# Attention and feed-forward on one core: the prologue's bias load, its stores and the second batch's projections are put in another order

## The chip, the core and the metric

One core of a Trainium2 chip runs the whole kernel. The metric is the device time of one execution in microseconds (us). The engines are TensorE (PE; the load of its weights is PEld), VectorE (DVE), ScalarE (ACT), GpSimd (POOL) and SyncE (SP), each with an instruction queue of its own; SP, ACT and POOL also issue DMAs.

## The reference

Two sequences (B = 2) of 1024 rows of 128 numbers pass a pre-norm attention with 16 heads of 8 and a feed-forward of 512, all in 32-bit floats:

```python
x = x + attn(layernorm(x))
x = x + ffn(layernorm(x))
def attn(x):
    q, k, v = x @ Wq.T + bq, x @ Wk.T + bk, x @ Wv.T + bv
    sim = einsum('bhid,bhjd->bhij', q, k) + rel_emb[bucket(i - j)] * SCALE
    sim = where(j > i, -inf, sim)
    return einsum('bhij,bhjd->bhid', softmax(sim), v) @ Wo.T + bo
def ffn(x):
    y = x + relu(x @ w1[0] + b1[0]) @ w2[0] + b2[0]
    return layernorm(y) * gamma + beta
```

The bias of a score depends only on i - j and the head, by a table of 32 buckets.

## The kernel before

**Groups and steps.** The work is cut into 8 groups g of 4 heads (4 groups of each batch), and a group into 12 steps. A step takes one block of 128 keys against up to 512 queries: `scores` (keys times queries), `biases` (adds the near biases TT), an exponential on ACT (line 743), and `values`, which sums probabilities times values on TensorE. The softmax's maxima must be known before a group's scores, so each group also has 42 jobs, its "units". A unit multiplies queries by keys on TensorE (line 1130); DVE then takes the maximum of each row, far units by `TENSOR_REDUCE` (line 883), near units with the bias table NBH added (line 890, one instruction and a short read-out for each head). Units 16 and 41 are "m" units: TensorE turns the maxima of half a group (line 1116), DVE copies them out (`mrow`, line 878), and SP moves them by a DMA into the operand QA (`move_m`, line 462). The first scores of a half wait for that DMA. Units use three banks of PSUM in turn, so TensorE can be up to three units ahead of DVE. The units of group g + 1 stand between the steps of group g. Group 0 has no group before it: its first units (OWN0 of them) run ahead of the first scores.

**Prologue of batch 0.** The order of each engine is written out by hand, in the program's text. DVE and ACT normalise 4 tiles of 128 rows at a time (`stats0`, `deviation`, `norm`), TensorE turns them (`task_t`, line 1046), ACT copies them back (`turned`, line 676), TensorE multiplies by Wq and Wk (`task_qk`, line 1052) and Wv (`task_v`, line 1058). Each query and key is kept as three bf16 parts: ACT writes the first part (`first_parts`, line 681), DVE forms the remainder, the second part and the third (`split`, lines 830, 832, 835); for the first 512 queries POOL forms the third (line 591). SP stores the parts to DRAM (`store` and `store_keys`, lines 445 and 454); from there `load_q` (SP, lines 408 and 412) and `load_k` (POOL or ACT, lines 420 and 424) load them in the layout of the units, QA and KA. A pair (b, c) is batch b, half c of its 1024 rows; all five stores of a pair count on one semaphore, s_qst[b][c].

**Biases.** `task_f` multiplies the table by one-hot rows into one bank, `bias_table` on DVE makes of it the reversed biases Fr and the two parts F16. SP stores both. ACT loads them back as `rev` (1 MB, in the tile PT, line 713) and `TL` (two transfers of 480 KB, in the tile OT, line 716). Eight `task_flip` turn `rev` into NBH by way of ACT and DVE (`copy_nbh`, lines 696 and 851); `copy_tt` on ACT makes TT of TL (line 705).

**Batch 1.** POOL normalises it (`second_batch_norm`, lines 574 to 579). Its projections stand between the first 17 units of group 0, Q and K of one half together (T_AT, QK_AT, V_AT). ACT writes its first parts and the whole values (line 684), POOL splits those (lines 608 to 612). They are stored on SP and first loaded for group 4. `keep_busy` multiplies zeros on TensorE, in three places: before the table, before the first turn, and 12 of them ahead of the first scores (line 1282).

## Time and profile before

| what | us |
|---|---|
| median of 3 runs | 344.32 (344.03 to 344.61) |
| profiled execution, whole | 342.63 |
| profiled execution, span | 340.8 |
| TensorE busy | 286.3 (84% of the span) |
| VectorE busy | 272.6 (80%) |
| ScalarE busy | 190.3 (56%) |
| GpSimd busy | 92.0 (27%) |

A span runs from the first to the last instruction; the execution's own time adds what lies around it. Shares are means over stages that have different limits, so a stage is read from its own stretch. A row of the chain names, for a stretch of time, the work that the last instruction hung on; a row of the timeline names when an engine or queue started something, how long it took and, in brackets, how long the engine had been idle before and what ended that. SPq, ACTq and POOLq are the DMA issues of an engine's queue: their time is that of issuing, not of moving.

### The profile page before, as it was taken

The page shows a single profiled execution, that of the slowest core. Times are in us where ns is not written, and L with a number is a line of the kernel's source. Part 1 is how long each engine was busy: PE and PEld are TensorE (multiplying, and loading weights), DVE is VectorE, ACT ScalarE, POOL GpSimd, SP SyncE. Part 2 cuts the span into 40 slices and gives each one's busy share as a digit, 9 for nine tenths or more (in the row PEclk, how much of TensorE's full clock was granted, in tenths as well). Part 3 has the DMA queues.
Part 4 walks back from the last instruction along what each step waited for, and adds up shares of the span by engine and source line. Part 5 has one row for each costly group of instructions (what it writes and reads, how often), then busy time and mean ns, then how long its engine had stood idle before and what let it go on. Part 6 is the DMA issues. An engine that isn't in the chain of part 4 may idle for free.

```text
span 340.8 us, 8308 instructions
## 1 busy us (share of the span) xinstructions
PE 286.3 (84%) x3224; PEld 129.0 (38%) x3224; DVE 272.6 (80%) x967; ACT 190.3 (56%) x264; POOL 92.0 (27%) x138
## 2 busy tenths in 40 slices
PE   8492987769998989998898999889899988999880
PEld 4151342222343344334334334423432443367650
DVE  5653556989899888988888989888899957838894
ACT  2433544386558556755766674685575468843230
POOL 6109999602020220201022022001200001615351
PEclk9967698969999999999999999999999999999997
DMA  7475417001010120102022222114221002000022
GB/s 217 131 205 145 132 38 236 17 2 38 21 56 4 56 56 3 53 7 57 0 57 56 34 64 55 35 25 87 56 34 26 9 14 37 4 4 13 0 63 62
DMA packets 16263, 18.80 MB, mean 55 GB/s; under 512 B 4576, under 2 KB 11872, under 8 KB 16096
## 3 DMA queue, kind: packets, MB, share of 16 engines
q1 hardware_dynamic: 13168, 12.10, 14.6%
q0 software_dynamic: 2400, 3.45, 3.5%
q10 hardware_dynamic: 656, 2.73, 2.7%
q8 instruction: 25, 0.41, 0.5%
q14 instruction: 14, 0.11, 0.1%
HBM read 11.81 MB, written 4.23 MB: 47 GB/s over the span
## 4 chain that ended last, share of the span: by engine, by line
PE 52%; DVE 22%; ACT 11%; issue 6%; DMA 4%; POOL 3%; SPq 1%; DVEq 0%; POOLq 0%
PE ps L1174 15%; PE ps L1130 12%; ACT PT L743 9%; DVE FM L883 8%; PE ps L1145 8%; PE ps L1162 7%; DVE junk L890 4%; PE ps L1052 3%; DMA qk_scratch<-QS 2%; PE ps L1207 2%; DVE st L947 2%; DVE U L1000 1%; PE ps L1116 1%; PE ps L1077 1%; DVE xnT L913 1%
## 5 line engine op out<-in xcount | busy, mean ns | idle before, releaser
L743 ACT ACTIVATE PT<-ps 128x1024 f32<-128x1024 f32 (+1 forms) x192 | 144.7, 814 | 92.2 <-PE ps L1162 87.3
L883 DVE TENSOR_REDUCE FM<-ps 128x1 f32<-128x512 f32 (+2 forms) x192 | 109.1, 616 | 12.8 <-PE ps L1130 12.3
L890 DVE CUSTOM_DVE_ANT_0 junk<-ps,NBH 128x256 bf16<-128x256 f32 (+1 forms) x256 | 90.2, 399 | 23.5 <-PE ps L1130 23.5
L1130 PE MATMUL ps<-KA,QA 56*128 56x256 bf16 (+3 forms) x544 | 96.5, 288 | 14.7 <-DVE FM L883 7.4
L1145 PE MATMUL ps<-QA,KA 58*128 58x512 bf16 (+3 forms) x384 | 77.7, 333 | 17.6 <-ACT PT L743 14.6
L1174 PE MATMUL ps<-PT,VG 128*16 128x512 f32 (+3 forms) x768 | 86.1, 493 | 0.1
L1130 PEld LDWEIGHTS ps<-KA,QA 56*128 56x128 bf16 x544 | 33.3, 95 | 99.8 <-DVE FM L883 42.1
L420 POOL DMA_DIRECT2D KA<-qk_scratch x30 | 16.4, 550 | 163.3 <-PE ps L1162 151.9
L1145 PEld LDWEIGHTS ps<-QA,KA 58*128 58x128 bf16 x384 | 24.8, 94 | 37.4 <-ACT PT L743 30.4
L1162 PE MATMUL ps<-TT,flb 128*32 128x176 f16 (+4 forms) x1152 | 38.4, 243 | 0.0
L1162 PEld LDWEIGHTS ps<-TT,flb 128*32 128x32 bf16 x1152 | 21.3, 96 | 17.1 <-issue 15.5
L1174 PEld LDWEIGHTS ps<-PT,VG 128*16 128x16 f32 x768 | 21.5, 97 | 6.1 <-ACT OT L748 2.3
L890 DVE DVE_READ_ACCUMULATOR2_ANT FM<- 128x1 f32 x256 | 20.7, 81 | 0.0
L641 POOL TENSOR_SCALAR tmp<-mv 128x4 f32<-128x4 f32 x8 | 2.3, 290 | 66.7 <-DVE mv L950 66.7
L1207 PE MATMUL ps<-QS,late_s 128*128 128x512 f32 x32 | 15.8, 611 | 0.8 <-ACT QS L773 0.8
L424 POOL DMA_DIRECT2D KA<-qk_scratch x30 | 15.5, 528 | 0.0
L1052 PE MATMUL ps<-xnT,early_s 128*128 128x512 f32 x16 | 13.0, 958 | 1.9 <-ACT xnT L676 1.9
L936 DVE RECIPROCAL xnT<-xnT 128x256 f32<-128x256 f32 (+1 forms) x4 | 10.1, 2537 | 0.0
L681 ACT ACTIVATE QS<-ps,early_s 128x512 bf16<-128x512 f32 x8 | 5.5, 692 | 8.2 <-PE ps L1052 8.2
L956 DVE TENSOR_TENSOR QS<-ps,X 128x512 f32<-128x512 f32 x4 | 2.7, 682 | 8.5 <-PE ps L1198 8.5
L748 ACT COPY OT<-ps 128x512 f32<-128x512 f32 x16 | 9.5, 592 | 0.0
L1046 PE MATMUL ps<-early_s,XN 128*128 128x128 f32 x16 | 4.0, 396 | 6.3 <-DVE XN L820 4.2
(98 smaller groups left out, 256.2 us busy)
## 6 DMA issues: line engine op xcount, KB each, us to landing
QA<-qk_scratch SPq DMA_DIRECT2D x64, 48.0 KB
KA<-qk_scratch POOLq DMA_DIRECT2D x30, 96.0 KB, 2.6
qk_scratch<-QS SPq DMA_DIRECT2D x12, 128.0 KB
qk_scratch<-QS SPq DMA_DIRECT2D x8, 192.0 KB
X<-in_x SPq DMA_DIRECT2D x4, 256.0 KB, 5.1
PT<-fr_scratch ACTq DMA_DIRECT2D x1, 1024.0 KB, 5.6
out<-U SPq DMA_DIRECT2D x4, 256.0 KB, 2.3
OT<-f_scratch ACTq DMA_DIRECT2D x2, 480.0 KB, 8.3
```

The source lines that it names most:

```text
L420: eng.dma_start(KA[64 * e:64 * e + 48, p, c, :, :].rearrange("r h n -> r (h n)"), bass.AP(qk_d, at + e * TILE, [[LINE, 2 * HD], [0, NPART] ...
L424: eng.dma_start(KA[64 * e + 48:64 * e + KS, p, c, :, :].rearrange("r h n -> r (h n)"), bass.AP(qk_d, at + e * TILE + 2 * HD * LINE, [[LINE ...
L743: nc.scalar.activation(PT[:, s % 3, 2 * q:2 * q + 2, off:off + w], ST[:, q, :, off:off + w], ACT.Exp).then_inc(s_exp, 1)
L883: nc.vector.tensor_reduce(FM[:, ib, heads[0]:heads[-1] + 1:2, piece], bank[:, 0:w * len(heads)].rearrange("p (h n) -> p h n", n=w), AX.X, ...
L890: last = nc.vector.tensor_tensor_reduce(junk[:, n % NSM, i, 0:w], bank[:, i * w:(i + 1) * w], nb[:, h, 256 - w:256], 1.0, NEG, ALU.add, AL ...
L936: own2(nc.vector.reciprocal(den, den))
L1052: nc.tensor.matmul(ps[:, BANK["QK"[qk], b, c], :], (wq_s, wk_s)[qk][:, :], xnT[:, b, c * IC:(c + 1) * IC], start=True, stop=True).then_inc ...
L1130: last = nc.tensor.matmul(SM[:, n % NSM, i * w + j - j0:i * w + j - j0 + nj], QA[r0:r0 + KS, p, ib // 4, q, (ib % 4) * 128:(ib % 4 + 1) * ...
L1145: last = nc.tensor.matmul(ST[:, q, e, off:off + w], KA[64 * e:64 * e + KST, p, jb // 4, q, (jb % 4) * 128:(jb % 4 + 1) * 128], QA[64 * e:6 ...
L1162: last = nc.tensor.matmul(ST[r0:r0 + 32, q, h % 2, off:off + n], flb[:, 32 * e:32 * e + 32], TT[:, hg, h, u0:u0 + n], start=False, stop=Tr ...
L1174: last = nc.tensor.matmul(OV[32 * h:32 * h + 2 * HD, off:off + w], VG[:, jb, g, h, :], PT[:, s % 3, h, off:off + w], start=(jb == 0), stop ...
L1207: last = nc.tensor.matmul(bank, w1_s[:, f * 128:(f + 1) * 128], tT[:, c % 2, :], start=True, stop=True)
```

## The change

- Two banks take the two halves of the bias table; the reversed one is multiplied first, the other behind the first turn. SP stores Fr and at once loads `rev`, ahead of all stores of queries and keys. The three operations that make F16 go from DVE to POOL. TL is loaded by SP behind `load_q(0, 0, 1)`.
- s_qst is split into one semaphore for queries and one for keys. ACT stores the second and third parts of the first 512 keys; POOL forms the third part of both halves of queries of batch 0.
- TensorE's first three `task_f`, the flips, V of batch 0 and `keep_busy` are in another order, and more zeros are multiplied early (10, 5 and 4); the 12 ahead of the first scores are gone.
- POOL takes the root of all eight tiles of batch 1 at once. ACT writes only the whole values of batch 1's Q and K, and POOL makes the first part too.
- Batch 1's projections stand one by one between the units (BATCH1_AT). In group 0 the first m unit comes ahead of units 14 and 15, and 21 jobs instead of 17 stand before the first scores.

```diff
+def order_of(g):
+    ks = list(range(NU - 1))
+    if g == 0:
+        ks.remove(M0)
...
 def stream():
     out = []
     for g in range(G):
-        for k in range(NU - 1):
...
-T_AT = {2: 0, 8: 1}
-QK_AT = {4: 0, 10: 1}
-V_AT = {13: 0, 15: 1}
+BATCH1_AT = {7: ("T", 0), 9: ("Q", 0), 10: ("K", 0), 12: ("V", 0), 13: ("T", 1), 15: ("Q", 1), 16: ("K", 1), 18: ("V", 1)}
 RECIP_AFTER = (6, 14, 22, 30)
-OWN0 = 17
+OWN0 = 21
...
-        STORED = 16 * (HP + NPART)
+        STORED_Q, STORED_K = 16 * HP, 16 * NPART
...
+            at = (2 * c + 1) * SIDE + b * 2 * GPB * TILE + a * HD * LINE
+            eng.dma_start(bass.AP(qk_d, at, [[TILE, 2 * GPB], [IC, HD * HP], [1, IC]]),
+                          QS[:, b, 1, a, c * IC:(c + 1) * IC]).then_inc(s_qst[b][c][1], 16)
         @block.sync
...
+            sp.dma_start(rev[:, :], bass.AP(fr_d, 0, [[H, 128], [1, 256 * H]])).then_inc(s_rev, 16)
+            sp.wait_ge(s_q1, 2)
+            store_keys(sp, 0, 0, 0)
+            store(0, 0, 0)
             sp.wait_ge(s_f, 2)
             for part in range(2):
                 sp.dma_start(bass.AP(f16_d, part * BW * H, [[H, 128], [128 * H, XC], [1, H]]),
                              F16[:, part, :, :]).then_inc(s_fst[1], 16)
-            def key_part(c, a):
-                ready, count = ((s_q1, 2 * c + 2), (s_mid, 2 * c + 2), (s_q3[0][1], c + 1))[a]
-                sp.wait_ge(ready, count)
-                store_keys(0, c, a)
-            key_part(0, 0)
-            key_part(0, 1)
-            store(0, 0, 0)
-            key_part(0, 2)
-            sp.wait_ge(s_qst[0][0], STORED)
+            sp.wait_ge(s_qst[0][0][0], STORED_Q)
             load_q(sp, 0, 0, 0)
-            key_part(1, 0)
+            sp.wait_ge(s_q1, 4)
+            store_keys(sp, 0, 1, 0)
             store(0, 1, 0)
-            key_part(1, 1)
-            key_part(1, 2)
-            sp.wait_ge(s_qst[0][1], STORED)
+            sp.wait_ge(s_mid, 4)
+            store_keys(sp, 0, 1, 1)
+            sp.wait_ge(s_q3[0][1], 2)
+            store_keys(sp, 0, 1, 2)
+            sp.wait_ge(s_qst[0][1][0], STORED_Q)
             load_q(sp, 0, 0, 1)
+            sp.wait_ge(s_fst[1], 32)
+            for part in range(2):
+                sp.dma_start(TL[64 * part:64 * part + 64, :],
+                             bass.AP(f16_d, part * BW * H, [[H, 64], [1, NEARU * H]])).then_inc(s_tl, 16)
             load_q(sp, 1, 1, 0)
+            move_m(0, 0, 0)
             load_q(sp, 1, 1, 1)
-            move_m(0, 0, 0)
             sp.dma_start(late_s[:, :], late).then_inc(s_late, 16)
             for c in range(2):
                 for qk in range(2):
...
+                pool.wait_ge(s_var, 4)
+                nc.gpsimd.tensor_scalar(tmp4[:, 8:16], mv[:, 8:16, 1], EPS, None, ALU.add).then_inc(s_p1, 1)
+                pool.wait_ge(s_p1, 1)
+                nc.gpsimd.tensor_tensor(rs[:, 8:16], tmp4[:, 8:16], mhalf[:, :], ALU.pow).then_inc(s_p1, 1)
+                pool.wait_ge(s_p1, 2)
             def second_batch_norm(k):
...
+                pool.wait_ge(s_mid, 2 * c + 1)
+                q = QS[:, 0, 0, :, c * IC:(c + 1) * IC]
+                nc.gpsimd.tensor_tensor(q[:, 2, :], R[0][:, 2 * c, :], q[:, 1, :], ALU.subtract).then_inc(s_lo, 1)
             ones(0)
...
-            pool.wait_ge(s_mid, 1)
-            q = QS[:, 0, 0, :, 0:IC]
-            nc.gpsimd.tensor_tensor(q[:, 2, :], R[0][:, 0, :], q[:, 1, :], ALU.subtract).then_inc(s_lo, 1)
+            pool.wait_ge(s_ff, 1)
+            nc.gpsimd.tensor_copy(F16[:, 0, :, :], Ff[:, :, :]).then_inc(s_p3, 1)
+            pool.wait_ge(s_p3, 1)
+            nc.gpsimd.tensor_tensor(Ff[:, :, :], Ff[:, :, :], F16[:, 0, :, :], ALU.subtract).then_inc(s_p3, 1)
+            pool.wait_ge(s_p3, 2)
+            nc.gpsimd.tensor_scalar(F16[:, 1, :, :], Ff[:, :, :], LSC, None, ALU.mult).then_inc(s_f, 1)
+            queries_lo(0)
             pool.wait_ge(s_zero, 3)
-            pool.wait_ge(s_qst[0][0], STORED)
+            pool.wait_ge(s_p2, 1)
+            pool.wait_ge(s_qst[0][0][1], STORED_K)
             load_k(pool, 0, 0, 0, s_ldk)
-            pool.wait_ge(s_p2, 1)
+            queries_lo(1)
+            second_batch_deviation()
             second_batch_norm(2)
             second_batch_norm(3)
             pool.wait_ge(s_rows, 16)
             add_bv(0)
             load_k(pool, 1, 1, 0, s_ldk)
-            pool.wait_ge(s_qst[0][1], STORED)
...
                 c, qk = k // 2, k % 2
                 q = QS[:, 1, qk, :, c * IC:(c + 1) * IC]
                 pool.wait_ge(s_r, k + 1)
+                nc.gpsimd.tensor_copy(q[:, 0, :], R[1][:, k, :]).then_inc(s_p0, 1)
+                pool.wait_ge(s_p0, 3 * k + 1)
                 nc.gpsimd.tensor_tensor(R[1][:, k, :], R[1][:, k, :], q[:, 0, :], ALU.subtract).then_inc(s_p0, 1)
-                pool.wait_ge(s_p0, 2 * k + 1)
+                pool.wait_ge(s_p0, 3 * k + 2)
                 nc.gpsimd.tensor_copy(q[:, 1, :], R[1][:, k, :]).then_inc(s_p0, 1)
-                pool.wait_ge(s_p0, 2 * k + 2)
+                pool.wait_ge(s_p0, 3 * k + 3)
...
             act.wait_ge(s_early, 16)
-            first_parts(0, 0)
-            act.wait_ge(s_fst[0], 16)
-            act.dma_start(rev[:, :], bass.AP(fr_d, 0, [[H, 128], [1, 256 * H]])).then_inc(s_rev, 16)
-            act.wait_ge(s_fst[1], 32)
-            for part in range(2):
-                act.dma_start(TL[64 * part:64 * part + 64, :],
-                              bass.AP(f16_d, part * BW * H, [[H, 64], [1, NEARU * H]])).then_inc(s_tl, 16)
+            first_parts(0)
             act.wait_ge(s_warm, 1)
             nc.scalar.activation(warm[:, :], eps[:, :], ACT.Exp).then_inc(s_warm, 1)
+            act.wait_ge(s_mid, 2)
+            store_keys(act, 0, 0, 1)
+            act.wait_ge(s_q3[0][1], 1)
+            store_keys(act, 0, 0, 2)
+            copy_nbh(0)
+            copy_nbh(1)
             turned(0, 1)
-            first_parts(0, 1)
-            for i in NBH_ACT:
+            copy_nbh(2)
+            first_parts(1)
+            for half in range(2):
+                copy_v(0, half)
+            for i in NBH_ACT[3:]:
                 copy_nbh(i)
-            copy_v(0)
             turned(1, 0)
             act.wait_ge(s_zero, 1)
-            act.wait_ge(s_qst[0][1], STORED)
+            act.wait_ge(s_qst[0][1][1], STORED_K)
             load_k(act, 0, 0, 1)
-            first_parts(1, 0)
+            whole(0)
+            copy_v(1, 0)
             turned(1, 1)
+            whole(1)
+            copy_v(1, 1)
             act.wait_ge(s_tl, 32)
             copy_tt(0)
-            first_parts(1, 1)
-            copy_v(1)
...
             dve.wait_ge(s_early, 16)
-            bias_table()
+            bias_rows()
             stats0(1)
-            nc.vector.tensor_copy(idb[:, :], idf[:, :]).then_inc(s_cst, 1)
             nc.vector.tensor_copy(flb[:, :], flp[:, :]).then_inc(s_cst, 1)
+            bias_columns()
+            stats0(2)
             for qk in range(2):
                 split(0, qk)
             norm(1)
-            for k in range(2, 4):
-                stats0(k)
-            for i in NBH_DVE:
-                copy_nbh(i)
+            copy_nbh(NBH_DVE[0])
+            stats0(3)
+            nc.vector.tensor_copy(idb[:, :], idf[:, :]).then_inc(s_cst, 1)
             for qk in range(2):
                 split(1, qk)
+            copy_nbh(NBH_DVE[1])
             def unit(g, p, k):
...
+            def second_batch(kind, half):
+                if kind == "T":
+                    if half == 0:
...
+                    task_qk(1, half, qk)
             pe.wait_ge(s_idle, 1)
-            keep_busy(5, 5)
+            pe.wait_ge(s_ov, 2)
+            keep_busy(7, 10)
             pe.wait_ge(s_tab, 16)
-            task_f()
-            keep_busy(5, 2)
+            task_f(1)
             pe.wait_ge(s_early, 16)
             task_t(0, 0)
-            task_qks(0, 0)
-            task_t(0, 1)
-            task_qks(0, 1)
-            pe.wait_ge(s_f, 2)
-            pe.wait_ge(s_ov, 2)
-            pe.wait_ge(s_cst, 2)
+            task_f(0)
+            for qk in range(2):
+                task_qk(0, 0, qk)
+            keep_busy(7, 5)
+            pe.wait_ge(s_mid, 1)
+            task_v(0, 0)
+            keep_busy(7, 4)
+            pe.wait_ge(s_cst, 1)
+            pe.wait_ge(s_ff, 1)
             pe.wait_ge(s_rev, 16)
             for i in range(4):
                 task_flip(i)
             pe.wait_ge(s_mid, 2)
-            task_v(0, 0)
+            task_t(0, 1)
+            for qk in range(2):
+                task_qk(0, 1, qk)
             task_v(0, 1)
             for i in range(4, 8):
                 task_flip(i)
@@ -1261,25 +1313,18 @@
             HALF_UNITS = {0: 0, min(k for k, u in enumerate(UNITS) if u[0] != "m" and u[1] >= 4): 1}
             pe.wait_ge(s_mid, 4)
+            pe.wait_ge(s_cst, 2)
             pe.wait_ge(s_nbh, len(NBH_ACT))
             pe.wait_ge(s_nbd, len(NBH_DVE))
-            for k in JOBS[:JOBS.index(OWN0)]:
-                if k in T_AT:
-                    task_t(1, T_AT[k])
-                if k in QK_AT:
-                    pe.wait_ge(s_vc, 2)
-                    task_qks(1, QK_AT[k])
-                if k in V_AT:
-                    if k == min(V_AT):
-                        pe.wait_ge(s_r, 2)
-                    task_v(1, V_AT[k])
+            for n, k in enumerate(order_of(0)[:OWN0]):
+                if n in BATCH1_AT:
+                    second_batch(*BATCH1_AT[n])
                 if k in HALF_UNITS:
                     operands(0, HALF_UNITS[k], 1)
                 job(0, 0, k)
             pe.wait_ge(s_r, 4)
             pe.wait_ge(s_vc, 4)
             nc.tensor.matmul(ps[0:64, 0, 0:64], flb[:, 0:64], flb[:, 0:64], start=True, stop=True).then_inc(s_pv, 3)
-            keep_busy(1, 12)
             pe.wait_ge(s_tt, 1)
             for q in range(2):
                 scores(0, 0, 0, q)
@@ -1306,15 +1351,12 @@
...
 FLIP_BANK = [6, 7, 0, 1, 6, 7, 0, 1]
-NBH_ACT, NBH_DVE = (0, 2, 4, 5, 6, 7), (1, 3)
+NBH_ACT, NBH_DVE = (0, 1, 2, 4, 5, 6), (3, 7)
```

SP, from its first store after the loads of the input. The names are tiles of the program: fr_scratch and f_scratch hold the biases in DRAM, PT is `rev`, qk_scratch the queries and keys. Before:

```order
L477 DMA fr_scratch<-Fr 128x3x16 [waits s_f]
L480 DMA f_scratch<-F 128x3x16 [waits s_f]
L480 DMA f_scratch<-F 128x3x16
L454 DMA qk_scratch<-QS 8x16x512 [waits s_q1]
L454 DMA qk_scratch<-QS 8x16x512 [waits s_mid]
L445 DMA qk_scratch<-QS 192x1x512 [waits s_lo]
L445 DMA qk_scratch<-QS 192x1x512
L454 DMA qk_scratch<-QS 8x16x512 [waits s_q30k]
L408 DMA QA<-qk_scratch 24x1024 [waits s_qst00]
```

and now:

```order
L488 DMA fr_scratch<-Fr 128x3x16 [waits s_f]
L490 DMA PT<-fr_scratch 128x4096 [waits s_fst0]
L442 DMA qk_scratch<-QS 8x16x512 [waits s_q1]
L462 DMA qk_scratch<-QS 192x1x512 [waits s_lo]
L462 DMA qk_scratch<-QS 192x1x512
L496 DMA f_scratch<-F 128x3x16 [waits s_f]
L496 DMA f_scratch<-F 128x3x16
L418 DMA QA<-qk_scratch 24x1024 [waits s_qst00q]
```

The load of `rev` stands second and waits only for its own store; the first keys' second and third parts are gone from this queue (they are on ACT's), and the stores of F16 are behind those of the queries.

TensorE, from far units of group 0 (L1130, L1182) to the first scores (L1145, L1197). Before:

```order
L1130 MATMUL ps<-KA,QA 128x384 [waits s_smf] x2
L1058 MATMUL ps<-early_s,xnT 128x128 x4
L1130 MATMUL ps<-KA,QA 128x384 [waits s_smf]
L1116 MATMUL ps<-idb,MC 8x128 [waits s_ms,s_smf]
L1116 MATMUL ps<-idb,MC 8x128 x3
L1281 MATMUL ps<-flb 64x64 [waits s_vc,s_r]
L1077 MATMUL ps<-idle 128x512 x12
L1145 MATMUL ps<-QA,KA 128x512 [waits s_exp,s_md0,s_tt]
L1145 MATMUL ps<-QA,KA 128x512
```

and now, from just behind the m unit:

```order
L1087 MATMUL ps<-xnT,early_s 128x512 [waits s_xt]
L1182 MATMUL ps<-KA,QA 128x384 [waits s_smf]
L1182 MATMUL ps<-KA,QA 128x128 [waits s_smf]
L1182 MATMUL ps<-KA,QA 128x128 x3
L1093 MATMUL ps<-early_s,xnT 128x128 [waits s_r]
L1093 MATMUL ps<-early_s,xnT 128x128 x3
L1182 MATMUL ps<-KA,QA 128x128 [waits s_smf]
L1182 MATMUL ps<-KA,QA 128x128 x3
L1182 MATMUL ps<-KA,QA 128x512 [waits s_smf] x2
L1327 MATMUL ps<-flb 64x64 [waits s_vc,s_r]
L1197 MATMUL ps<-QA,KA 128x512 [waits s_exp,s_md0,s_tt]
L1197 MATMUL ps<-QA,KA 128x512
```

K and V of batch 1's second half (L1087, L1093) stand between single units, four more units (17 to 20) stand ahead of the first scores, and the 12 products of zeros (L1077) are gone.

## Rows read from the trace of the kernel before

**Rows 1.** the page of the whole kernel, busy tenths in 40 slices of 8.5 us
```profile
PE   8492987769998989998898999889899988999880
PEclk9967698969999999999999999999999999999997
```

**Rows 2.** the chain that ended last, from 0 to 100: start, us, what
```profile
9.33 3.49 PE ps L1052 x4
16.99 8.36 DMA qk_scratch<-QS
25.98 0.76 POOL KA L420
47.81 2.70 PE ps L1077 x12
51.08 0.39 PE ps L1145 x2
71.64 1.74 DMA QA<-mrow
```

**Rows 3.** timeline of the DMA issues: start, us taken to issue, queue, line, what
```profile
12.85 0.34 ACTq L713 DMA_DIRECT2D PT<-fr_scratch  x1
13.23 1.17 ACTq L716 DMA_DIRECT2D OT<-f_scratch  x2
16.99 0.61 SPq L454 DMA_DIRECT2D qk_scratch<-QS  x1
29.55 1.80 SPq L454 DMA_DIRECT2D qk_scratch<-QS  x2
34.73 1.52 SPq L408 DMA_DIRECT2D QA<-qk_scratch  x4
```

**Rows 4.** DMA issues from 0 to 50: KB each, median us to landing
```profile
PT<-fr_scratch ACTq DMA_DIRECT2D x1, 1024.0 KB, 5.6
OT<-f_scratch ACTq DMA_DIRECT2D x2, 480.0 KB, 8.3
fr_scratch<-Fr SPq DMA_DIRECT2D x1, 12.0 KB, 1.7
```

**Rows 5.** timeline of TensorE, start, us taken, line, what
```profile
1.21 2.31 PE L1077 MATMUL ps<-idle 128*128 128x512 bf16 x5 [1.21 <-DVE idle L801]
3.83 2.74 PE L1038 MATMUL ps<-table_s 32*128 32x16 f32 x12 [0.30 <-DMA table_s<-in_table]
18.77 1.22 PE L1052 MATMUL ps<-xnT,early_s 128*128 128x512 f32 x1 [0.68 <-ACT xnT L676]
41.44 1.96 PE L1052 MATMUL ps<-xnT,early_s 128*128 128x512 f32 x4 [0.34 <-ACT xnT L676]
30.69 0.40 PE L1130 MATMUL ps<-KA,QA 56*128 56x128 bf16 x4 [4.54 <-DMA KA<-qk_scratch]
```

**Rows 6.** a stretch of 1 us: busy us (x instructions) of PE, PEld, DVE, ACT, POOL, clock, DMA
```profile
22.00:23.00 1.00, 1.00 (x4) 0.34 (x3) 0.00 (x0) 0.42 (x1) 0.00 (x0) 0.69 0.87 296
```

**Rows 7.** timeline of VectorE, GpSimd and ScalarE, columns as in rows 5
```profile
13.01 0.43 DVE L832 CAST QS<-PT 128x512 bf16<-128x512 f32 x1
13.52 1.15 POOL L591 TENSOR_TENSOR QS<-PT,QS 128x512 bf16<-128x512 f32 x1 [7.23 <-DVE QS L832]
14.35 0.60 DVE L832 CAST QS<-PT 128x512 bf16<-128x512 f32 x1
14.99 0.69 DVE L835 TENSOR_TENSOR QS<-PT,QS 128x512 bf16<-128x512 f32 x1
30.03 3.14 POOL L579 TENSOR_SCALAR XN<-X,mv,rs 128x128 f32<-128x128 f32 x4
41.20 1.95 ACT L705 COPY TT<-OT 128x960 f16<-128x960 f16 x1
```

**Rows 8.** two stretches of the units, columns as in rows 6
```profile
31.20:48.50 17.30, 14.33 (x65) 6.93 (x66) 10.35 (x44) 8.92 (x13) 16.96 (x23) 0.75 0.36 98
51.70:71.00 19.30, 14.12 (x148) 5.00 (x145) 16.72 (x61) 8.90 (x11) 13.65 (x23) 0.90 0.34 105
```

129 lines of the change are left out of this document (67 added, 62 removed).

## The prediction

> **What bounds the kernel now.** I read the page's slices first. TensorE is busy nine tenths or more from the tenth slice on; among the first nine, up to some 77 us, most have holes, and its clock is below full in several of them [rows 1]. The change works only there, so I followed the chain of waits through the first 100 us and looked at each of its long pieces in the timeline.
>
> Three stretches stand out. **First**, everything up to the first product of queries and keys at 30.69, for which TensorE sat idle 4.54 us until the keys' load landed [rows 5]. The chain goes back from there to POOL's loads at 25.98, and from these through 8.36 us in which nothing on the chain but the stores to DRAM was under way, from the last store's issue at 16.99 [rows 2]. That store had company: ACT had just issued the 1 MB of `rev` at 12.85 and twice 480 KB of TL at 13.23 [rows 3], which took 5.6 and 8.3 us themselves [rows 4]. The second half's stores had no such neighbour: the last two were issued from 29.55 to 31.35, and SP, which waits for them all, went on at 34.73 [rows 3]; that is 4.3 us from the start of the last one. **Second**, the units ahead of the first scores, 30.69 to 51.08 [rows 2, 5]. From 31.2 to 48.5 DVE works 10.35 of 17.3 us and TensorE 14.33, at a mean clock of 0.75 [rows 8]: neither is full, TensorE is nearer, and DVE waits whenever a whole block of batch 1's projections stands between two units. It ends in 2.7 us of zeros, under which the maxima travel [rows 2]. **Third**, the early part of group 0, 51.7 to 71.0: DVE is busy 16.72 of 19.3 us [rows 8], the maxima of the second half leave it near 70.9, and the chain passes through their DMA to TensorE [rows 2]. There DVE sets the pace.
>
> **Stretch one: 30.7 becomes about 23.8.** The ten zeros start when the memset of their bank is done, near 1.8; at 0.46 each (five took 2.31 [rows 5]) they end at 6.4. Half of the table's products is half of 2.74 [rows 5], so the reversed biases are ready near 7.9, half a microsecond later than now, although the table itself has been there since 3.8. SP stores them (1.7 [rows 4]) and issues `rev` near 9.9; at its 5.6 us [rows 4] it lands by 15.5. Its successors, the flips, come then, before the second turn, and not after it as now.
>
> Queries and keys: now they take 3.49 us for two products [rows 2], and the same pair takes 1.96 at 41.44 [rows 5]. That is 1.2 against 2.4 GHz, though the clock's row shows full speed for the early part, too. From 18.77 [rows 5] TensorE worked without a gap and its clock rose within the stretch 22 to 23, which shows 0.69 granted [rows 6]: some 3.9 us of gapless work. The change gives it gapless work from 1.8 on. I take 2.4 GHz, so 1.5 us less, for this pair; the table's other half stands in between, where TensorE now idles for 0.7 us, and costs nothing at either rate that matters. Keys' first part: 13.5 becomes 12.0. DVE's third part ended at 15.68 [rows 7], 2.15 behind it, so 14.2. Now it is stored at 16.99 by SP, behind the queries; then it is stored by ACT at once: 2.8 us earlier. The landing of the stores shrinks from 8.36 to 4.3, since only `rev` is ahead of them and TL is far behind: 18.5 instead of 25.35. From there to the first product it was 5.3 us (the loads are unchanged, 25.37 to 30.69): 23.8. **6.9 us gained.** What is late next is the rest of batch 0: `rev` by 15.5, four flips, the second turn and its four products, four flips and DVE's second split, which I put at 22.7; it is hidden by 1 us only.
>
> The three operations of F16 go to POOL, whose queue is idle for 7.23 us there [rows 7]; TL is wanted only at the first scores. ACT's wait for DVE before its two stores delays its first flip copy by nothing, since `rev` lands later. The two semaphores cost nothing.
>
> The Trainium skill, SBUF — State Buffer, "SBUF: two separate sides", speaks against more work on POOL: a GpSimd operation and a VectorE one with two inputs in SBUF, or in a fast mode, shut each other out for a whole instruction. This trace agrees in size: the cast at 14.35 took 0.60 beside POOL's 1.15 us operation and 0.43 at 13.01 [rows 7]. By that rule the keys' third part could wait a full 1.15 us, and the forecast below would be 334.5.
>
> **Stretch two: 51.1 becomes about 42.5.** DVE's work is 10.35 [rows 8] and four more units (17 to 20). In the second stretch of rows 8 a job is about 0.65 (16.72 over some 26 jobs), so 2.7 with the reads of longer rows: a floor of 13.0, scores not before 36.9 plus ACT's tail. TensorE's work: 14.33 less the 0.75 us of zeros in that stretch is 13.6; with four units of 0.4 (the first took 0.40 [rows 5]) 15.2, at the same mean clock. The turn of batch 1's first half waits for POOL: loads issued until 21.1, third part 1.15, root 1.3, norm 3.14 [rows 7], so 26.7 where TensorE arrives near 26: 1 us. The order's tail hangs on ACT: the copy of the last values 0.6, then TT with 1.95 [rows 7], on which the first scores wait; before, TT was copied while units ran. Sum: 23.8 + 15.2 + 1.0 + 2.5 = 42.5. The maxima's DMA now has six jobs and two projections above it; it cost 2.7 us of zeros and is hidden. **8.6 us gained in all up to here**, 1.7 of it in this stretch, with four units more done. The second half's operands are wanted by unit 12: stores issued until 25 (SP now waits for POOL's third part of the queries, which is behind POOL's loads), landed 4.3 later, loads 5.3 more, 34 or so; TensorE gets there at about 33. Close, but inside the 1 us.
>
> Ends: with TensorE never in the way, 36.9 + 2.5 = 39.4, 3.1 us better. With it at 1.2 GHz throughout, 15.2 x 0.75 / 0.5 = 22.8, so 50.1, 7.6 us worse. I take the mean clock of before, because long projections between short units look alike in both programs.
>
> **Stretch three.** 2.7 us of DVE's work are gone from a stretch that DVE fills to 87%; I count 2.4. POOL has four more casts of 0.6 for batch 1; they hide behind the fact that those parts are loaded only for group 4. ACT has four operations less. Everything behind group 0 has the same order, and nothing there waits for a clock time, so the lead is kept.
>
> **Sum.** 8.6 + 2.4 = 11.0 us. The profiled execution took 342.63 and would take 331.6; the median is 1.7 above it, so I forecast 344.3 - 11.0 = **333.3 us**.
>
> **Rivals.**
> - *The lead of stretch one is lost among the units.* One projection after each unit or two keeps TensorE working in small pieces, and its clock was half for nearly all of 30 to 39 in this trace too. For: among the first ten slices several show 6 to 8 tenths of clock [rows 1]. Against: it rose by itself once it had work. At 50.1 for the scores the gain is 1.0 + 2.4: 340.9; halfway, 337. Chance 0.19 for 337.5 to 343.5.
> - *Slower: the second half's operands come last.* Everything they need is now in one line: POOL's loads, then the queries' third part, then SP's stores, then ACT and SP loads, and ACT's writes of batch 1 behind its wait. If landing stays at 8.4 (that is, if `rev` and many small packets of the stores were the cause, not TL), first unit 14.2 + 8.4 + 5.3 = 27.9, SP's second stores out at 28.5, landed 36.9, loaded 42.2. Behind it are 5 units, the m unit, four projections and TT: some 9 + 2.5, scores at 53.7; with TensorE at 1.2 GHz 3 us more. That is 2.6 + 3 - 2.4 = 3.2 slower: 347.5. It decides the sign when the second operands land after about 41 and TensorE is slow. Against: the second stores' 4.3 us. Chance 0.07.
> - *It does nothing:* the holes move but DVE and TensorE stay as late. 344.3, chance 0.03; the stretch of 8.36 us makes it unlikely.
>
> **How the numbers follow.** Forecast case 0.71, the partial one 0.19, none 0.03, slower 0.07. A change of 0.2% (0.7 us) is about what can be told from none. So faster 0.90, same 0.03, slower 0.07. The range: 3.1 below by the good end of stretch two, 330.0; above it takes in the port's 1.15, four us of stretch one if its landing is not shortened, and half of the partial case: 340.0. Slower and the worse half of the partial case are left out.
>
> **What would show it.** In the new trace: the two products of queries and keys in about 2 us near 9 to 11; `rev` landed by 15.5; POOL's key loads near 18.5; first product of units near 23.8; unit 12 not waiting over 1 us for its operands; first scores near 42.5 and released by TT on ACT; no zeros before them; maxima of the second half out near 59.5; from there on the same pace as now. It would be wrong if the stores still took over 6 us to land, if TensorE stayed at 1.2 GHz from the first unit to the scores, or if DVE idled more than 3 us in group 0.

## The result, and the profile after

The changed kernel took 340.74 us (median of 20 executions, 335.82 to 342.9) where the one before took 344.00 (20, 342.29 to 346.41). The ratio is 0.985, with a 95% interval from 0.982 to 0.989; like the ratios in the table below, it leaves out executions more than 1.5% above the fastest of the same kernel, which are 9 of the changed kernel's 20 and none of the other's, while medians count all of them (their ratio is 0.991). The kernel is faster, by 1 to 1.5%: right in sign, less than half the 11.0 us forecast, and outside the range, whose upper end was 340.0.

The profiled execution has a span of 337.1 us instead of 340.8. The page of the changed kernel, the two rows that answer to [rows 1]:

```profile
PE   6966878689998888989988898999899889999880
PEclk9595696759999999999999999999999999999997
```

The holes are still there, and the clock's second and fourth digits are 5 now. The chain of waits of the changed kernel, which answers to [rows 2] (start, us, what):

```profile
9.34 3.73 PE ps L1087 x4
...
13.80 1.28 ACT L742
...
16.29 4.62 DMA qk_scratch<-QS
...
21.57 0.77 POOL KA L430
...
27.60 3.15 POOL XN L593 x4
30.89 1.10 PE ps L1081 x4
...
33.97 6.38 DMA KA<-qk_scratch
...
46.48 1.83 ACT TT L734
48.36 0.39 PE ps L1197 x2
...
66.61 1.79 DMA QA<-mrow
```

The stores land in 4.62 us instead of 8.36, as forecast. The normalisation of batch 1 (L593) and its turn stood on the chain of the kernel before, too (from 30.03 to 34.35, not among [rows 2]). New are 6.38 us in which nothing on the chain but the load of the second half's keys is under way. TensorE's timeline, which answers to [rows 5]:

```profile
7.54 0.63 PE L1081 MATMUL ps<-early_s,XN 128*128 128x128 f32 x4 [1.07 <-DVE XN L852]
9.27 3.78 PE L1087 MATMUL ps<-xnT,early_s 128*128 128x512 f32 x4
26.56 0.80 PE L1182 MATMUL ps<-KA,QA 56*128 56x128 bf16 x6 [3.84 <-DVE NBH L885]
30.89 1.09 PE L1081 MATMUL ps<-early_s,XN 128*128 128x128 f32 x4 [0.80 <-POOL XN L593]
32.74 2.05 PE L1087 MATMUL ps<-xnT,early_s 128*128 128x512 f32 x2 [0.22 <-ACT xnT L703]
40.40 0.33 PE L1182 MATMUL ps<-KA,QA 56*128 56x384 bf16 x1 [0.84 <-DMA KA<-qk_scratch]
48.36 0.39 PE L1197 MATMUL ps<-QA,KA 58*128 58x512 bf16 x2 [1.54 <-ACT TT L734]
```

Five landmarks can be read from such timelines, and I use them for every run below: the first unit; unit 12 (the first product 384 wide, the first that reads keys of the second half); the first scores; the second half's maxima (their copy `mrow` on VectorE); and the same copy for group 1. From that last one to the end of the span it is 240.3 to 240.6 us in all 19 profiles, so nothing behind it matters.

| kernel | first unit | unit 12 | first scores | maxima | group 1's | span | median, runs | ratio to before (95%) |
|---|---|---|---|---|---|---|---|---|
| before | 30.69 | 44.90 | 51.08 | 70.50 | 100.51 | 340.8 | 344.0 | |
| changed | 26.56 | 40.40 | 48.36 | 65.46 | 96.70 | 337.1 | 340.74, 20 | 0.985 (0.982-0.989) |
| e1_zeros | 25.14 | 39.49 | 48.81 | 66.03 | 96.12 | 336.5 | 339.15, 6 | 0.987 (0.982-0.992) |
| e2_load_first | 26.66 | 40.29 | 48.36 | 65.60 | 96.72 | 337.1 | 338.68, 6 | 0.983 (0.979-0.987) |
| e3_split_dve | 25.89 | 40.43 | 51.12 | 68.28 | 98.79 | 339.4 | 342.20, 6 | 0.986 (0.980-0.991) |
| e4_before_tl | 28.77 | 41.39 | 52.70 | 71.72 | 102.84 | 343.1 | 345.03, 12 | 1.000 (0.997-1.003) |
| e5_tl_behind | 24.86 | 38.40 | 46.42 | 63.67 | 94.91 | 335.3 | 338.68, 6 | 0.983 (0.980-0.986) |
| e6_warm | 27.17 | 42.38 | 53.08 | 68.40 | 98.43 | 338.8 | 341.04, 7 | 0.991 (0.988-0.994) |
| e7_warm_tl | 26.43 | 39.47 | 50.17 | 66.61 | 96.64 | 337.0 | 337.83, 6 | 0.983 (0.980-0.986) |
| e8_m1_zeros | 24.54 | 38.98 | 46.93 | 64.07 | 95.09 | 335.5 | 341.82, 12 | 0.993 (0.990-0.995) |
| e9_tt_first | 25.08 | 39.45 | 48.52 | 65.66 | 95.92 | 336.3 | 339.48, 4 | 0.986 (0.980-0.993) |
| e10_own17 | 27.04 | 40.90 | 51.63 | 72.26 | 102.30 | 342.7 | 345.08, 10 | 1.002 (0.998-1.005) |
| e11_all_mended | 26.85 | 39.96 | 47.87 | 65.87 | 96.51 | 336.9 | 336.58, 4 | 0.978 (0.973-0.983) |
| e12_mended_warm | 25.01 | 38.42 | 46.18 | 64.04 | 94.08 | 334.5 | 336.77, 4 | 0.980 (0.973-0.987) |
| e13_norm_early | 26.59 | 40.78 | 50.34 | 67.47 | 97.91 | 338.3 | 342.29, 10 | 0.992 (0.988-0.996) |
| e14_mended_norm | 24.58 | 37.61 | 45.34 | 62.54 | 92.57 | 333.0 | 334.69, 4 | 0.973 (0.968-0.979) |
| e15_mended_own17 | 24.57 | 37.95 | 45.35 | 68.27 | 98.65 | 339.1 | 340.89, 9 | 0.990 (0.988-0.993) |
| e16_zeros_in_wait | 24.80 | 37.93 | 45.74 | 62.50 | 92.55 | 332.9 | 335.02, 4 | 0.974 (0.968-0.979) |
| e17_own17_z12 | 25.04 | 38.86 | 48.95 | 68.26 | 98.29 | 338.7 | 341.70, 10 | 0.994 (0.990-0.997) |

By stretches, the lead of the changed kernel is 4.1 us at the first unit, 4.5 at unit 12, 2.7 at the first scores, 5.0 at the maxima and 3.8 at group 1's.

One profile is one execution, and the clock falls differently in each: the profiles show by which way time goes, and what a kernel is worth is read from its executions. The runs come from several chips, each beside executions of the kernel before with medians of 344.0 to 344.7. So two rows are compared by their ratios, and where the intervals overlap no difference is shown. e2 is a warning: its landmarks are those of the changed kernel, and its median is still 2.1 us lower.

### The profile page after: what moved, and what is told of

Read it like the earlier page. It is cut to its first block, busy times and chain, and to the rows that moved or that the text cites. A ratio compares the mean times of both kernels' runs of the same rounds, so it can differ in the third digit from the quotient of the medians.

```text
span 337.1 us, 8306 instructions
## 1 busy us (share of the span) xinstructions
PE 288.0 (85%) x3224; PEld 129.3 (38%) x3224; DVE 273.7 (81%) x963; ACT 188.2 (56%) x260; POOL 96.0 (28%) x144
## 3 DMA queue, kind: packets, MB, share of 16 engines
q0 software_dynamic: 2400, 3.45, 3.7%
## 4 chain that ended last, share of the span: by engine, by line
PE 53%; DVE 18%; ACT 12%; issue 6%; DMA 5%; POOL 4%; ACTq 1%; SPq 0%; DVEq 0%; POOLq 0%
PE ps L1226 16%; PE ps L1182 13%; ACT PT L775 9%; PE ps L1197 8%; PE ps L1214 8%; DVE FM L918 6%; DVE junk L925 2%; DMA KA<-qk_scratch 2%; PE ps L1259 2%; PE ps L1087 2%; DVE st L982 2%; DVE U L1035 1%; DMA qk_scratch<-QS 1%; PE ps L1168 1%; DMA X<-in_x 1%
## 5 line engine op out<-in xcount | busy, mean ns | idle before, releaser
L1182 PE MATMUL ps<-KA,QA 56*128 56x256 bf16 (+3 forms) x544 | 98.6, 293 | 13.9 <-DVE FM L918 6.1
L1197 PE MATMUL ps<-QA,KA 58*128 58x512 bf16 (+3 forms) x384 | 78.8, 337 | 18.1 <-ACT PT L775 14.4
L1182 PEld LDWEIGHTS ps<-KA,QA 56*128 56x128 bf16 x544 | 33.4, 96 | 100.8 <-DVE FM L918 38.4
L1197 PEld LDWEIGHTS ps<-QA,KA 58*128 58x128 bf16 x384 | 25.1, 94 | 38.3 <-ACT PT L775 30.6
L1087 PE MATMUL ps<-xnT,early_s 128*128 128x512 f32 x16 | 12.1, 874 | 1.0 <-ACT xnT L703 0.9
L809 ACT ACTIVATE QS<-ps,early_s 128x512 f32<-128x512 f32 x8 | 5.5, 687 | 6.6 <-PE ps L1259 6.5
L1107 PE MATMUL ps<-idle 128*128 128x512 bf16 x19 | 7.2, 540 | 1.9 <-DVE ps L834 1.9
```

The lines of the kernel that those rows point to most:

```text
L1087: nc.tensor.matmul(ps[:, BANK["QK"[qk], b, c], :], (wq_s, wk_s)[qk][:, :], xnT[:, b, c * IC:(c + 1) * IC], start=True, stop=True).then_inc ...
L1182: last = nc.tensor.matmul(SM[:, n % NSM, i * w + j - j0:i * w + j - j0 + nj], QA[r0:r0 + KS, p, ib // 4, q, (ib % 4) * 128:(ib % 4 + 1) * ...
L1197: last = nc.tensor.matmul(ST[:, q, e, off:off + w], KA[64 * e:64 * e + KST, p, jb // 4, q, (jb % 4) * 128:(jb % 4 + 1) * 128], QA[64 * e:6 ...
```

## Experiments on the prologue

**The zeros ahead of the turn.** In the profile of the changed kernel TensorE stood idle 1.07 us ahead of the first turn, and the pair of queries and keys took 3.78 us at 1.2 GHz. The windows of that profile (busy us and instructions of PE, PEld, DVE, ACT, POOL; then the granted clock):

```profile
8.00:9.00 1.00, 1.00 (x8) 0.91 (x6) 0.81 (x7) 0.80 (x2) 0.00 (x0) 0.68 0.29 43
9.00:10.00 1.00, 1.00 (x3) 0.73 (x4) 0.62 (x4) 0.03 (x1) 0.26 (x2) 0.50 0.00 0
```

e1_zeros fills that hole:

```diff
             task_f(1)
+            keep_busy(7, 4)
             pe.wait_ge(s_early, 16)
```

> The changed kernel with four more products of zeros between the table's first half and the first turn, where TensorE idled for 1.07 us. Theory (the idle time let the clock fall back to 1.2 GHz just ahead of Q and K, which then took 3.78 us): the pair takes about 2.0 us, its first parts and all that hangs on them come 1.5 us earlier, the first unit near 25 instead of 26.6; the total gains 0 to 1.5 us. Rival (the clock falls for another reason, or the first unit hangs on something else): the pair stays at 3.5 us or more, or the first unit stays at 26.6.

The pair took 1.98 us and the first unit came at 25.14, but unit 12 waited 1.84 us for the keys and the scores came no earlier. Over all profiles the zeros do what they are for: with these four the pair took 1.98 us in all eight (e1, e7, e11, e12, e14 to e17), without them 3.13 to 3.78 in seven of nine (1.98 in e5 and e8). The hole is not the whole cause, though: in e6 and e10 TensorE's timeline shows no gap from 1.89 to the pair, the table's products took 1.46 us instead of 0.84 there, and the pair took 3.78 all the same. The gain stops at the next wait.

**ACT's key load ahead of its copy of the third turn.** 

```diff
-            turned(1, 0)
             act.wait_ge(s_zero, 1)
             act.wait_ge(s_qst[0][1][1], STORED_K)
             load_k(act, 0, 0, 1)
+            turned(1, 0)
```

> The changed kernel with ACT's load of the second half's keys ahead of its copy of batch 1's first turn. Theory (the units stall at unit 12, 40.4, because this load was issued at 32.1, behind a copy that waits for POOL's norm, though its stores had landed by 28.7): it is issued near 28.7 and lands before TL crowds it, by 34; unit 12 near 36 to 38, first scores near 45 instead of 48.4, total 2 to 3.5 us less than the changed kernel. Rival (batch 1's projections on a slow TensorE set the pace, the load only happened to be later): unit 12 comes at 39.5 or later, total within 1 us of the changed kernel.

All five landmarks stayed within 0.15 us. The load left ACT only 0.7 us earlier, at 31.34, when the keys' own stores had landed (the last, issued at 27.58, took 3.69 us). Unit 12 no longer waited for keys. The chain now passes through batch 1's projections at 1.2 GHz (2.05 us at 34.28, 2.00 at 36.86), which came out just as late: the rival. And TensorE now waited 1.59 us for ACT's copy of the turn, which stands behind the load, where it had waited 0.22.

**The third part of the second queries back on VectorE.**

```diff
-                if qk:
+                if k:
                     dve.wait_ge(s_mid, k + 1)
...
             load_k(pool, 0, 0, 0, s_ldk)
-            queries_lo(1)
```

> The changed kernel with the third part of the second queries back on DVE, behind its second part, as before. Theory (DVE's subtraction took 2.41 instead of 0.69 us because POOL's DMA issues and its own subtraction ran beside it, and the last copy of the near biases stood behind it): the two subtractions take 0.7 us each, the copy ends near 25.3 instead of 26.2, SP's stores of the second half go out 1 us earlier; total 0 to 1 us less. Rival (the slow instruction is slow whatever runs beside it, or the keys' load ends at the same time anyway): one of the two subtractions still takes over 2 us, or the first unit stays within 0.4 us of 26.6.

Both subtractions took 0.69 us, as the theory had it (the last section comes back to them), and the first unit came at 25.89, with 0.3 us of the gain from a shorter pair of queries and keys (3.45). SP issued the last stores at 23.53 instead of 26.33 and ACT's load went out at 30.47, but it now travelled beside TL (SP, 30.05). The chain of this run:

```profile
30.47 0.67 ACTq L430
...
32.37 8.02 DMA KA<-qk_scratch
```

8.02 us instead of 6.38: the transfer started 1.6 us sooner and landed at the same moment, unit 12 at 40.43 as before. It had more of TL beside it, and POOL's loads for group 1 started sooner, too (34.26 instead of 36.22); this run does not tell the two apart. TensorE had then waited 2.16 us, and the stretch behind took 10.69 us instead of 7.96.

**TL's move alone, in the kernel before.** 

```diff
-            act.wait_ge(s_fst[1], 32)
-            for part in range(2):
-                act.dma_start(TL[64 * part:64 * part + 64, :],
...
             load_q(sp, 0, 0, 1)
+            sp.wait_ge(s_fst[1], 32)
+            for part in range(2):
+                sp.dma_start(TL[64 * part:64 * part + 64, :],
...
```

> The kernel before, with nothing changed but that TL (twice 480 KB) is loaded by SP behind the second half's queries instead of by ACT beside the first stores. Theory (the first stores took 8.36 us to land because TL moved at the same time): they land 4 to 5 us after the last issue, the first unit comes near 27.5 instead of 30.7, and the total falls by 2 to 3 us. Rival (the stores' own 1 KB pieces and the 1 MB of rev were the cause): they still take 7 us or more.

The landing of the stores shrank to 3.3 us (18.39 to 21.66), and the first unit came 1.9 us sooner; it waited for VectorE's split now and no longer for keys. That confirms the term on the landing. At the first scores nothing was left of it:

```profile
47.94 0.23 PE L1281 MATMUL ps<-flb 128*64 128x64 bf16 x1 [3.15 <-ACT VG L694]
48.50 4.26 PE L1077 MATMUL ps<-idle 128*128 128x512 bf16 x11 [0.33 <-DMA QA<-mrow]
```

TensorE waited 3.15 us and its zeros then ran at 1.2 GHz: 4.26 us instead of 2.70 [rows 2]. Ratio 1.000, where 2 to 3 us had been expected.

**TL behind the first load for group 1, and ACT's load first.**

```diff
             load_q(sp, 0, 0, 1)
-            sp.wait_ge(s_fst[1], 32)
-            for part in range(2):
-                sp.dma_start(TL[64 * part:64 * part + 64, :],
...
             load_q(sp, 1, 1, 0)
+            sp.wait_ge(s_fst[1], 32)
+            for part in range(2):
+                sp.dma_start(TL[64 * part:64 * part + 64, :],
...
-            turned(1, 0)
             act.wait_ge(s_zero, 1)
             act.wait_ge(s_qst[0][1][1], STORED_K)
             load_k(act, 0, 0, 1)
+            turned(1, 0)
```

> The changed kernel with TL's two loads moved behind the queries of group 1's first half on SP, and ACT's load of the second keys ahead of its copy. Theory (unit 12 waits for the second half's keys, whose load takes 6.4 to 8 us because 960 KB of TL and the loads for group 1 move beside it): the load lands 3.5 us after it is issued, near 35.5; unit 12 near 37 to 38; first scores near 46; total 2 us under the changed kernel. Rival (TensorE's projections at 1.2 GHz are as late as the load, so they take over): unit 12 at 39.3 or later, scores no earlier than 47.8, total within 1 us.

No wait at unit 12, which stood 13.54 us behind the first unit instead of 13.84. So the rival is right here: with the keys in time, TensorE's own projections at 1.2 GHz were as late as the load had been. The scores at 46.42 owe 1.7 us to the first unit, where queries and keys took 1.98 us by chance of the clock. The ratio, 0.983, is that of e2 and within the changed kernel's interval: no gain is shown.

## Experiments on the clock

e6_warm has zeros from the first unit on; e7_warm_tl adds the edits of e1 and e5.

```diff
+            keep_busy(7, 8)
             for n, k in enumerate(order_of(0)[:OWN0]):
...
                 job(0, 0, k)
+                keep_busy(7, 2)
```

> The changed kernel with zeros multiplied into the free bank 7: eight ahead of the first unit and two behind each of the 21 jobs before the first scores, so that TensorE's clock stays at 2.4 GHz. Theory (the clock at 1.2 GHz through the projections costs the units about 5 us): projections take 1.0 instead of 2.05 us each, but the zeros add 0.43 each job; unit 12 still waits for its keys near 40.3, so the scores come only 0 to 1 us earlier. If the load is not what holds unit 12, it comes by 37 and the scores by 46.

The clock was 1.00 from 16 to 62, and the third turn's projections took 1.02 us each instead of 2.05. Yet the scores came at 53.08, 25.9 us behind the first unit instead of 21.8: two zeros behind each of 21 jobs cost more than the clock gave, and unit 12 waited 2.23 us for its keys. The expected 0 to 1 us did not come.

> E5 and E6 together, with the four zeros ahead of the first turn as well. If load and clock are the two causes of the missing time in the units, each hidden by the other, then only this one gains: unit 12 near 35 to 36, first scores near 43 to 44 (forecast 42.5), total 4 us or more under the changed kernel. If either was not a cause, it gains no more than 1.5 us over the better of the two.

The ratio is 0.983, as for e5, and the median 0.9 us below e5's: the joint gain of 4 us or more is not there. The zeros made unit 12 to the scores 10.70 us long; what they cost there, the following stretch gave back in part (16.44 for 17.10). So these runs do not tell what the units would take at full clock without the zeros' own cost.

e8_m1_zeros has zeros in `scores`, in one place: ahead of those that wait for the second half's maxima.

```diff
                 if q == 0 and jb == 0:
+                    if g == 0 and ic == 1:
+                        pe.wait_ge(s_exp, 2 * s + 1)
+                        keep_busy(0, 6)
                     pe.wait_ge(s_md[ic], 32 * g + 32)
```

> The changed kernel with six products of zeros ahead of the first scores of group 0's second half, where TensorE waits for the maxima (66 to 68.4) at 1.2 GHz. Theory (the 1.2 us that were lost between 68 and 94 against the kernel before went to the clock, which stayed at 1.2 GHz from 63 to 76.7): the clock rises by 70, and the lead at 94 over the kernel before grows from 3.8 to 5 us or more; total 1 to 2 us less than the changed kernel. Rival (DVE or the zeros themselves hold it up): total same or up to 1 us more.

The clock was 0.99 from 68 to 95, and still maxima to group 1's took 31.02 us; it was 31.24 in the changed kernel and 30.0 to 30.3 in ten other profiles. But the zeros were themselves in the way. They ran at 1.2 GHz:

```profile
65.77 2.74 PE L1107 MATMUL ps<-idle 128*128 128x512 bf16 x6
```

and the scores started 4.37 us behind the maxima instead of 2.98. From these scores to group 1's maxima it was 26.65 us, against 28.26 in the changed kernel. The same eight products of probabilities and values, in the changed kernel (a row of its chain; 1.91 in the timeline) and in e8:

```profile
72.80 1.84 PE ps L1226 x8
```

```profile
72.15 1.05 PE L1229 MATMUL ps<-PT,VG 128*16 128x512 f32 x8
```

So 1.6 us were won by the clock and 1.4 lost to the zeros, and the ratio is no better.

## Experiments on the units and the tail

**TT ahead of the last values' copy.**

```diff
             whole(1)
-            copy_v(1, 1)
             act.wait_ge(s_tl, 32)
             copy_tt(0)
+            copy_v(1, 1)
```

> The changed kernel with ACT's copy TT ahead of its copy of the last values (copy_v(1, 1)), as it stood relative to them before the change. In the changed kernel the first scores wait 1.54 us on TT alone, after everything else they need. Theory (the tail on ACT is in series with the units): TL has landed by about 40, TT is copied between 41 and 44, the values' copy ends near 46.6 and the first scores start near 46.9 instead of 48.36; span 335.6 to 336.0 instead of 337.1, if the lead is kept. Rival (the lead is given back in group 0, where VectorE sets the pace): scores at 46.9 but the second half's maxima leave VectorE at 65.5 as now, span 337 +- 0.3. A second rival: TL lands only after 42, so the copy of the values is held and the scores gain under 0.5 us.

The wait for TT only changed its name: TensorE waited 1.20 us for the copy of the values, which now stood behind TT, and Q of the second half took 2.02 us at 1.2 GHz. The scores came at 48.52, ratio 0.986: nothing gained.

**17 jobs instead of 21 ahead of the scores.**

```diff
-BATCH1_AT = {7: ("T", 0), 9: ("Q", 0), 10: ("K", 0), 12: ("V", 0), 13: ("T", 1), 15: ("Q", 1), 16: ("K", 1), 18: ("V", 1)}
+BATCH1_AT = {7: ("T", 0), 9: ("Q", 0), 10: ("K", 0), 12: ("V", 0), 13: ("T", 1), 14: ("Q", 1), 15: ("K", 1), 16: ("V", 1)}
-OWN0 = 21
+OWN0 = 17
```

> The changed kernel with 17 instead of 21 jobs ahead of the first scores (the last three pieces of the second batch at places 14, 15, 16); the four units go back into group 0. It prices the part of the change that moves units. The prediction held that four units cost about 2.7 us of stretch two and give 2.4 us back behind it: then the first scores start 1.5 to 2.7 us earlier (45.7 to 46.9), the second half's maxima leave VectorE 0 to 1 us later than 65.5, and the span is 337 to 338. Rival (the units were moved into idle time of VectorE, which waits for the projections anyway): the first scores start less than 1 us earlier, since the projections and TT set them, and the span is 338.5 to 339.5, about 2 us longer.

Neither theory had this. With less to do the scores came 3.3 us **later**, at 51.63, and the median was 345.08: the whole gain of the change was gone. The timeline:

```profile
40.90 0.33 PE L1182 MATMUL ps<-KA,QA 56*128 56x384 bf16 x1 [2.94 <-DMA KA<-qk_scratch]
42.50 2.07 PE L1087 MATMUL ps<-xnT,early_s 128*128 128x512 f32 x2 [0.24 <-ACT xnT L703]
45.02 2.08 PE L1087 MATMUL ps<-xnT,early_s 128*128 128x512 f32 x2
47.46 1.67 PE L1093 MATMUL ps<-early_s,xnT 128*128 128x128 f32 x8
```

In the changed kernel the same three took 1.13, 1.13 and 1.16. TensorE had waited 2.94 us for the keys, and the clock was at half afterwards. The table holds the same pattern in kernels with 21 jobs and no zeros between them: with a wait at unit 12 of 0 to 0.94 us, unit 12 to the scores took 7.7 to 8.1 us (seven profiles); with 1.07, 1.84, 2.16 and 3.17 it took 9.1, 9.3, 10.7 and 9.6. Such a wait is paid for twice, though not in proportion to its length.

**Four repairs together**: the zeros of e1, TL behind `load_q(1, 1, 0)`, ACT's load first, TT first.

> The changed kernel with four repairs together: four products of zeros between the third turn of the table and the first tiles (so TensorE has no idle microsecond before queries and keys), TL loaded behind load_q(1, 1, 0), ACT's key load ahead of its copy of the third turn, TT ahead of the last values' copy. If the causes found one by one add up: queries and keys in 1.98 us, first unit near 24.9, unit 12 near 38.4, first scores near 45.0, span 334.0 to 334.8; median about 3 us below the changed kernel's. Rival (another wait of nearly the same lateness takes each one's place, TensorE's low clock above all): first scores at 46.4 as with the moved load alone, span 335.3 or more. If the gain of queries and keys is luck of the clock rather than the zeros' doing, they take 3.5 us or more here.

Queries and keys took 1.98 us and nothing waited for keys. This profile is the slowest of the four executions (338.77; the others 336.2 to 336.7): the clock was low from 6.2 to 10.3, though TensorE had had no gap since 1.89, and the pair began 2.4 us later than in e14. The ratio is 0.978 against 0.985, some 2 us, and the two intervals just overlap. Two waits are new. TensorE waited 1.52 us for ACT's copy of the turn, which now stands behind ACT's load; and on the way to the second half's maxima a small cast on VectorE, 0.17 us in the changed kernel, was held up:

```profile
63.12 1.77 DVE L939 CAST MC<-NM 128x16 bf16<-128x16 f32 x1
```

(1.40 in e12; the last section comes back to it).

e12_mended_warm adds eight zeros ahead of the first unit:

```diff
+            keep_busy(7, 8)
             for n, k in enumerate(order_of(0)[:OWN0]):
```

> The same with eight more products of zeros directly ahead of the first unit, in time in which TensorE waits for VectorE or the keys' load (3.8 us in the changed kernel), and none among the units. It asks whether the low clock of 26 to 38 in the changed kernel comes from that wait. If so: clock at 1.0 for the first units and perhaps for the projections at 32 to 36 (1.02 us each instead of 2.05), first scores 1 to 2.5 us before those of the run without these zeros. Rival (the clock falls from the small pieces among the units themselves, whatever was ahead): the projections still take 2.05, the scores start within 0.3 us of that run or up to 0.5 later, as the zeros may hold the first unit back.

The eight zeros kept the clock at full speed to the first units, and still the projections behind the turn took 2.05 us; TensorE had waited 1.19 us for POOL and 1.98 for ACT in between. So the low clock from 30 on (0.57 from 30 to 38, after 1.00 from 25 to 30) does not need the wait ahead of the first unit; it came behind those waits and small pieces. The ratio, 0.980, is that of e11 within the intervals.

**POOL's norm early.** For 6.95 us POOL waits for the first keys' stores, so the root (now of four tiles at a time) and the norm of the first four fit there:

```diff
             queries_lo(0)
+            second_batch_deviation(2)
+            pool.wait_ge(s_xn, 2)
+            second_batch_norm(2)
...
             queries_lo(1)
-            second_batch_deviation()
-            second_batch_norm(2)
+            second_batch_deviation(3)
             second_batch_norm(3)
```

> The changed kernel, in which POOL takes the root of the second batch's first four tiles and normalises them (norm, 3.1 us) while it would otherwise wait for the first keys' stores, 14.6 to 21.6; the other four tiles as before. Chain theory: the third turn no longer waits for POOL (0.80 us in the changed kernel) and comes near 30.1, ACT's key load leaves at 31.3 (the keys' own stores land then) instead of 32.07, unit 12 starts 0.7 earlier relative to the first unit (13.1), first scores about 1 us earlier, span 336 to 336.3 if queries and keys take the same 3.8 us as in the changed kernel's profile. Clock theory: TensorE's pace sets everything, unit 12 stays 13.8 behind the first unit and the span at 337. A second rival: POOL is done with both halves 3 us earlier, so its loads of group 1's keys start near 32.5 and travel beside the second half's load, which then takes over 7 us instead of 6.4: unit 12 14.5 or more behind the first unit, nothing gained or 1 us lost.

e14_mended_norm is e11 with this edit:

> The same early norm on top of the kernel with the four repairs (zeros, TL behind load_q(1, 1, 0), ACT's key load first, TT ahead of the last values), in which TensorE waited 1.09 and 1.52 us for POOL's norm and for ACT's copy of the turn, and its median was 336.6. Chain theory: both waits go to under 0.5 us, the first scores come 1 to 2 us earlier relative to the first unit (19.0 to 20.0 instead of 21.0), median 335.0 to 335.8. Clock theory: the pieces among the units run at 1.2 GHz anyway and the median stays at 336.6 +- 0.5. Second rival as above (POOL's earlier loads for group 1 get in the way of the second half's keys): unit 12 waits over 1 us for keys, median 337 or more.

e13 went by the second rival. The wait for POOL was gone and TensorE reached unit 12 at 37.6, 2 us early, but POOL's loads for group 1 now started at 32.52 and SP's TL at 30.98:

```profile
33.14 7.59 DMA KA<-qk_scratch
```

The keys landed at 40.73, 0.4 us later than in the changed kernel though the load had started 0.8 sooner; a wait of 3.17 us, the low clock behind it, ratio 0.992. The same edit in e14, with TL out of the way, is the fastest kernel here, with e16: 334.69, ratio 0.973 (0.968 to 0.979), some 4 us below the changed kernel by the ratios, 6 by the medians, and over 9 below the one before.

It did not go by the chain theory, though. The wait for POOL was gone, but the one for ACT's copy, behind ACT's load, grew from 1.52 to 2.07 us:

```profile
31.67 2.05 PE L1090 MATMUL ps<-xnT,early_s 128*128 128x512 f32 x2 [2.07 <-ACT xnT L706]
```

and the scores stood 20.8 us behind the first unit, not 19.0 to 20.0 (21.0 in e11). What this profile gained over e11's behind the first unit lies behind the scores (17.20 us to the maxima for 18.00): POOL was done with its additions before the cast of the maxima, which took 0.17 us again. The ratios of e11 and e14, 0.978 and 0.973, overlap in their intervals.

e15_mended_own17 is e11 with the edit of e10:

> The kernel with the four repairs and 17 jobs instead of 21 ahead of the first scores. If it was the 2.94 us wait for keys, and the low clock behind it, that made the 17 jobs slow, the wait is under 1 us here, the projections behind unit 12 run at 2.4 GHz (1.13 us each), the first scores come 2 to 2.7 us earlier relative to the first unit than with 21 jobs (18.3 to 19.0 instead of 21.0), the second half's maxima 2.3 to 3.5 later behind them, and the median is 336.5 to 338. If the four units themselves were what counted (VectorE has idle time ahead of the scores and none behind), the first scores gain under 1 us and the median is 339 or more.

With no wait for keys the projections ran at 1.12 to 1.16 us again: the low clock of e10 did come with the wait. But the scores stood 20.8 us behind the first unit with 17 jobs and 21.0 with 21 (e11), and the ratio is 0.990: the rival's two figures. The four units cost nothing ahead of the scores, since TensorE waits for ACT anyway (1.55 us in e15). Behind the scores they cost 4.9 us (22.92 against 18.00 in e11), but not by their work alone: the granted clock was 0.52 there against 0.79, and e11 had the held cast in it. Between e11 and e15 the medians differ by 4.3 us, between changed kernel and e10 by 4.3 too.

**The zeros that the change took away.** The first line is e16's edit to e14, the second e17's to e15:

```diff
+            keep_busy(2, 6)
             pe.wait_ge(s_r, 4)
             pe.wait_ge(s_vc, 4)
...
+            keep_busy(1, 12)
             pe.wait_ge(s_tt, 1)
```

> The best version so far (four repairs and the early norm, 334.69) with six products of zeros behind the 21st job, where TensorE waits 1.21 us for ACT's copy of the last values; they take 1.3 us at 2.4 GHz. Theory (the zeros that the change removed kept the clock up for group 0): the clock from the first scores to the second half's maxima is over 0.85 instead of 0.73, the stretch takes 16.0 to 16.7 us instead of 17.2, median 333.5 to 334.2. Rival (the clock falls in group 0 by its own small pieces and waits, whatever was ahead): stretch 17.2, median 334.7 +- 0.6.

> The kernel with the four repairs and 17 jobs, with the 12 products of zeros of before back at their place ahead of the first scores, where they cost 2.7 us at 2.4 GHz (first scores 48.0 instead of 45.35). If they kept the clock up: the stretch from the first scores to the second half's maxima takes 19.0 to 19.6 us at a clock of 0.85 or more instead of 22.9 at 0.52, the maxima leave at 67.0 to 67.6 instead of 68.3, median 340.0 to 340.5: the removal of the zeros cost 3.5 us in one place and gave 2.7 in the other. Rival (the clock of that stretch is luck, or set by the projections' end): 22 to 23 us again, maxima at 70 to 71, median 343 or more.

The same stretch, first scores to maxima, with 154 matmuls in each (columns as in [rows 6]): before, e15 without zeros, e17 with them.

```profile
51.10:70.50 19.40, 14.21 (x154) 5.24 (x154) 16.22 (x58) 8.40 (x10) 14.19 (x24) 0.91 0.36 111
```

```profile
45.40:68.30 22.90, 19.40 (x154) 6.78 (x154) 16.45 (x60) 9.05 (x11) 16.67 (x27) 0.52 0.32 97
```

```profile
48.90:68.30 19.40, 14.68 (x154) 5.27 (x154) 16.27 (x60) 8.45 (x10) 13.97 (x24) 0.83 0.29 92
```

VectorE and ACT do the same work, TensorE is busy 19.40 us for it or 14.7: the zeros do keep the clock up behind them, 3.6 us of stretch. The mean clock of the whole span says so beyond these two profiles: 0.931 to 0.943 over the nine executions of e15, 0.941 to 0.954 over the ten of e17. But the scores came 3.6 us later (0.5 of it there at the first unit already), so the maxima leave at 68.27 and 68.26, not at 67.0 to 67.6, and the median is 341.70, not 340.0 to 340.5 (e15: 340.89). In e16 the clock rose from 0.73 to 0.84 and the stretch shrank from 17.2 to 16.8, with the scores 0.2 us later relative to the first unit: 335.02 against 334.69, no difference. The 11-point rise of the clock was worth 0.4 us there, not 0.5 to 1.2.

## Why the prediction was right or wrong

**Stretch one: 4.1 us instead of 6.9.**
- *Landing of the stores, 8.36 to 4.3: right* (4.62; with TL alone moved 3.3).
- *Queries and keys 1.5 us shorter: wrong.* "The change gives it gapless work from 1.8 on" failed twice. The turn waits for VectorE's norm, whatever TensorE multiplies before, which left a hole of 1.07 us; filling it gave 1.98 us in eight profiles of eight. And gapless work from 1.89 on did not by itself bring 2.4 GHz to the pair: in e6 and e10 there was no gap and it took 3.78.
- *The keys' third part stored at 14.2, 2.8 us earlier: wrong,* 16.29, 0.7 earlier. It was ready at 15.75, 1.5 us late by the pair; the other 0.5 is ACT's own queue, where the reload of its table (13.80, 1.28 us) comes first, then the store of the second part (15.06), which takes 1.19 us to issue. I had counted neither.
- *Port conflict 1.15 us: not where I looked.* The first keys' subtraction took 0.69 (15.06). It was the second one that was held (last section). The 0.17 us by which the cast at 14.35 was longer [rows 7] was thin ground for "agrees in size".
- *Rest of batch 0 hidden by 1 us:* it was not hidden in this profile; NBH's last copy, behind the held subtraction, released the first unit at 26.56.

**Stretch two: 1.4 us lost instead of 1.7 gained.** The term that failed is "15.2 at the same mean clock", beside 3.5 us of waits. TensorE was busy 17.2 us of 21.8, at a granted 0.71 (0.78 over the same stretch before), and waited 4.6. Of the 2.0 us more of work 0.4 is a slip: the 14.33 was read from 31.2 on, and TensorE had been busy 0.40 us since the first unit at 30.69. The other 1.6 came with the lower clock. The single waits that I had named, for POOL (0.80 for 1.0), for the second keys (0.84 for "inside the 1 us") and the tail of TT, were about right; three waits of 0.3 us for VectorE at the first units were missing.

What I had not seen is that two chains of equal length run through this stretch. One lies outside TensorE: POOL's load, root, norm, turn, ACT's copy and only then ACT's load of 6.4 us. The other is TensorE's own projections at 1.2 GHz, which came out as late when the keys were there in time (e2 13.63, e5 13.54 us from first unit to unit 12, for 13.84). Unit 12 stood 13.0 to 14.5 us behind the first unit in all profiles of the changed order but e6, whose zeros hold it back. The rival that lost the lead among the units had 0.19; that is what happened, by waits that pull the clock down as well as by small pieces. Its price of 340.9 lies near the 340.74 by luck: it had the scores at 50.1 (48.36) and nothing lost behind them.

**Stretch three: 2.3 us gained, 2.4 forecast: right in size.** At equal clock (0.83 and 0.84) four units are worth 2.6 us there (e17 against e16, 19.3 and 16.8), and with 21 jobs the lower clock cost 0.4 (e14 against e16, 0.73 for 0.84). What I had not foreseen is that the removed zeros cost clock at all (0.73 for 0.91). With 17 jobs this is dear: 3.6 us (e15 against e17). So the move of the units also shielded the stretch from the loss of the zeros. VectorE idled 3.4 us of the 17.1 there, over the 3 us that I had named as a sign of being wrong: it did not set the pace alone.

**Behind it the lead was to be kept: 1.2 us was lost** between the maxima and group 1's; the clock was at 0.50 from 68 to 76 in the changed kernel and 0.65 in the one before. The profiles sort by it. Over the whole stretch, 31.1 to 31.2 us go with a mean clock of 0.82 (changed, e2, e4, e5), 30.4 to 30.6 with 0.84 or 0.85 (e3, e11, e13, e15), and 30.0 to 30.3 with 0.86 to 0.89 (the ten others); only e8 does not fit. In e8 full clock made the part behind the scores 1.6 us shorter, and its own zeros took 1.4 of them back. So "nothing there waits for a clock time" left out TensorE's clock. Why it rose later in this profile than in e1's is not shown.

**Sum:** 4.1 - 1.4 + 2.3 - 1.2 = 3.8 us, against a span 3.7 shorter. Of the 7.2 us missing from 11.0, 2.8 are stretch one, 3.1 stretch two, 0.1 stretch three and 1.2 the lead behind it. Without the four moved units the kernel is as slow as before (e10): the prologue's lead of 3.7 us is given back behind the late keys of the second half and, without the zeros, by the clock. One small reading was off and nothing hangs on it: behind the ninth slice TensorE is busy eight to nine tenths, not nine throughout [rows 1]. The moved units without the new prologue were not run.

## What to carry to other kernels

A lead is worth what the next wait leaves of it: look for every chain that ends within 1 us of the one you shorten, and repair them together. An early norm took the wait for POOL away in e13 and in e14; alone it brought the keys 0.4 us later and a wait of 3.17 us, with TL out of the way it had no such cost. A repair can also move a wait: ACT's load ahead of its copy freed the keys and made TensorE wait 1.5 to 2.1 us for the copy. Where TensorE's clock follows its waits, price a wait at its length and again as slower work behind it; and ask of every filler that you take away what runs at full clock because of it, and of every one that you add whether it stands in time that is idle: in e8 and e17 the zeros cost about what they gave. Work moved into time in which an engine waits anyway was the surest gain: four units ahead of the first scores were free and returned 4.3 us.

## What the runs showed of the hardware

**VectorE held up through GpSimd's next operation.** VectorE's subtraction of two operands in SBUF took 0.69 us when it began some 0.06 us ahead of POOL's second pair of DMA issues, in eleven profiles (in e1 at 22.01, the issues at 22.07; in e6 it began 0.61 us ahead and took as long), and 2.30 to 2.41 when it began 0.4 to 0.5 us into them, in four (changed, e13, e14, e16). In the changed kernel, VectorE and then POOL:

```profile
23.23 2.41 DVE L867 TENSOR_TENSOR QS<-PT,QS 128x512 bf16<-128x512 f32 x1
```

```profile
22.86 1.03 POOL L434 DMA_DIRECT2D KA<-qk_scratch  x2
23.91 1.17 POOL L600 TENSOR_TENSOR QS<-PT,QS 128x512 bf16<-128x512 f32 x1
```

It ended 0.56 us after POOL's subtraction (25.08), so it was held through that one. The issues alone do not do it: in e3, where no POOL subtraction follows them, it began 0.66 us into the same pair and took 0.69.

```profile
22.91 0.69 DVE L866 TENSOR_TENSOR QS<-PT,QS 128x512 bf16<-128x512 f32 x1
```

Why a subtraction that starts 0.6 to 0.7 us ahead of POOL's still loses to it is not shown. The Trainium skill, SBUF — State Buffer, "SBUF: two separate sides", has a pair of ports that one engine holds for a whole instruction. The trace agrees in kind, at 1.6 to 1.7 us rather than the 1.15 that I took for one.

The cast of the maxima in e11 shows a longer hold. POOL ran sixteen additions (into X, line 643) back to back there, the last of them ending at 64.85, and the cast, started at 63.12, ended at 64.89. In e12, e2 and e5 (1.40, 0.35 and 0.24 us for 0.17) it also ended 0.03 us behind POOL's last addition; in the changed kernel it began 0.1 us ahead of that end and took 0.17. So one operation of VectorE can be held through a whole row of GpSimd's, here on the way to the maxima that TensorE waits for.

**The clock's row is silent at the start.** The row shows 1.00 in every window up to 13 us of the profile before, where the pair took 3.49 us; it took 1.98 at 2.4 GHz. Durations of equal instructions tell the clock where the row does not.

**Small stores are slow in company.** The two 12 KB stores of the biases' parts landed in 1.7 us before, as the reversed ones did [rows 4], and in 4.2 in the changed kernel, where they go out behind the queries' stores.

**Spread.** The changed kernel's 20 executions lie 7 us apart, the kernel's before 4: the pair of queries and keys alone takes 1.98 to 3.78 us in nine profiles of kernels that are alike up to it, and this can be a part of it.
